# The attribute bias of an edge MLP as a 65th row of a matmul, and its relu in one instruction

## The reference, cut to what matters

```
ei   = concatenate([x[src], edge_attr], axis=-1)      # 256 + 64 values per edge
core = maximum(ei @ W1 + b1, 0.0) @ W2 + b2           # (320 x 256), then (256 x 256)
gate = sigmoid(ei @ Wg + bg)                          # (320 x 256)
agg  = segment_sum(gate * core, dst)
out  = layernorm(agg + x) * gamma + beta
```

## Time and profile before

| | |
|---|---|
| time, median of 3 runs | 3865.31 us (3860.82 to 3867.19) |
| the profiled execution | 3845.83 us, its span 3844.1 us |
| TensorE busy | 3249.5 us, 85% of the span |
| VectorE, GpSimd, ScalarE busy | 2816.0, 2085.0, 1883.4 us |
| mean granted TensorE clock | 0.925 of full speed |

### The profile page before, as it was taken

How to read it: one execution, slowest core, us unless ns; L and a number is a source line. 1 busy time by engine, 2 the same in 40 slices (tenths; PEclk the granted TensorE clock), 3 DMA queues, 4 the chain that set the end, 5 groups by cost and what they waited for, 6 DMA issues and landing times. The chain is left out here.

```text
span 3844.1 us, 56581 instructions
## 1 busy us (share of the span) xinstructions
PE 3249.5 (85%) x14868; PEld 2617.9 (68%) x14868; DVE 2816.0 (73%) x7894; ACT 1883.4 (49%) x5403; POOL 2085.0 (54%) x2118
## 2 busy tenths in 40 slices
PE   5999925588577799666999997999999999999875
PEld 4888824477465466333777775888878787878664
DVE  5666758699588466695666665898989898989742
ACT  3777715466333111132333332566666666666555
POOL 3667600376277566233333332767767676767567
PEclk8999969899799899755999998999999999999998
DMA  4788739644277222175333333887868686868665
GB/s 139 242 247 248 237 108 321 194 131 129 68 219 208 87 88 87 30 219 157 101 115 108 118 107 98 239 236 212 251 201 251 198 250 203 252 200 248 198 215 167
DMA packets 677311, 684.76 MB, mean 178 GB/s; under 512 B 73152, under 2 KB 631284, under 8 KB 676896
## 3 DMA queue, kind: packets, MB, share of 16 engines
q1 hardware_dynamic: 592456, 484.44, 40.4%
q0 software_dynamic: 68160, 181.21, 17.4%
q10 hardware_dynamic: 16380, 15.49, 1.2%
HBM read 401.66 MB, written 283.11 MB: 178 GB/s over the span
## 5 line engine op out<-in xcount | busy, mean ns | idle before, releaser
L2812 PE MATMUL s_i_bank<-s_i_messages,s_i_equal 128*128 128x256 f32 x1200 | 360.0, 383 | 5.6 <-DMA s_i_messages<-h,table_row 5.4
L621 POOL DMA_INDIRECT s_i_messages<-h,table_row x300 | 306.5, 1022 | 98.5 <-issue 78.7
L621 POOL DMA_INDIRECT s_i_messages<-h,table_row_b x300 | 308.0, 1027 | 90.1 <-issue 79.7
L931 POOL TENSOR_TENSOR n_powers<-n_powers,neg_half 128x8 f32<-128x8 f32 (+3 forms) x164 | 268.4, 1637 | 160.2 <-DVE n_powers L896 116.1
L856 ACT ACTIVATE n_z<-gamma_bc,n_powers 128x256 f32<-128x256 f32 x320 | 175.0, 594 | 362.0 <-POOL n_powers L931 362.0
L815 PE MATMUL s_n_bank<-w,n_xt 128*128 128x256 f32 x1280 | 305.7, 382 | 16.7 <-DMA n_xt<-in_x_t 16.7
L833 PE MATMUL s_n_bank<-w_out,n_ht 128*128 128x256 f32 x1280 | 313.9, 390 | 4.7 <-ACT n_ht L843 4.4
L824 PE MATMUL s_n_bank<-n_x3t,w_in 128*128 128x256 f32 x1280 | 302.5, 379 | 0.0
L2841 DVE SCALAR_TENSOR_TENSOR s_i_y<-s_i_bank,s_i_scale,acc 128x256 f32<-128x256 f32 x600 | 285.1, 476 | 0.3 <-PE s_i_bank L2812 0.2
L833 PEld LDWEIGHTS s_n_bank<-w_out,n_ht 128*128 128x128 f32 x1280 | 249.0, 196 | 46.2 <-ACT n_ht L843 11.1
L815 PEld LDWEIGHTS s_n_bank<-w,n_xt 128*128 128x128 f32 x1280 | 245.2, 192 | 51.3 <-DMA n_xt<-in_x_t 17.1
(11 more groups left out here) (448 smaller groups left out, 9244.8 us busy)
## 6 DMA issues: line engine op xcount, KB each, us to landing
h<-s_i_y SPq DMA_DIRECT2D x600, 128.0 KB, 3.9
n_xt<-in_x_t SPq DMA_DIRECT2D x160, 256.0 KB
out<-n_w SPq DMA_DIRECT2D x160, 256.0 KB
s_i_equal<-eq_tab SPq DMA_DIRECT2D x600, 64.0 KB, 3.9
x<-s_x_rows SPq DMA_DIRECT2D x100, 256.0 KB
out<-s_a_hs SPq DMA_DIRECT2D x100, 128.0 KB, 3.0
proj_dst<-s_a_hd SPq DMA_DIRECT2D x100, 128.0 KB
h<-s_h_rows SPq DMA_DIRECT2D x50, 256.0 KB, 3.7
```

The lines of the kernel that those rows point to most:

```text
L621: return net.nc.gpsimd.indirect_dma_start(out, None, table, bass.IndirectOffsetOnAxis(index, 0))
L931: self.nc.gpsimd.tensor_tensor(v[:, 8 + b0:8 + b1], v[:, b0:b1], self.net.neg_half[:, 0:b1 - b0], ALU.pow).then_inc(self.powered, 1)
L2812: nc.tensor.matmul(banks[r % 4][:, 0:D], EQ[q % NM][:], M[q % NM][:], start=True, stop=True).then_inc(summed, 1)
```

## The change

The bias of the MLP's first product goes into the product over the attributes, as it is in the gate already. `net.w_m1e` gets a 65th row, which is loaded with the bias; `hidden` multiplies it with all 65 rows of the attribute tile, whose last row is ones; the wait for those ones moves from `gate` to `hidden`. `relu` no longer has a bias, so one instruction over 512 values per partition takes the place of two over 256. The bias no longer needs its columns, and `net.cols` has two columns of biases where it had three; the list of loads keeps its 27 entries, but the entries behind `w_m1e` move by one place up to the former column load, and so change queues.

```
-        self.w_m1e = sb("w_m1e", [self.DE, D])
+        self.w_m1e = sb("w_m1e", [self.DE + 1, D])
...
-        self.col_names = ["b1", "bm1", "b_in"]
-        self.cols = sb("cols", [P, 3, C])
+        self.col_names = ["b1", "b_in"]
+        self.cols = sb("cols", [P, 2, C])
...
-            (net.w_m1[:], chunks(a["wm1"][0:D, :])), (net.w_m1e[:], a["wm1"][D:D + net.DE, :]),
+            (net.w_m1[:], chunks(a["wm1"][0:D, :])), (net.w_m1e[0:net.DE, :], a["wm1"][D:D + net.DE, :]),
+            (net.w_m1e[net.DE:net.DE + 1, :], a["bm1"].unsqueeze(0)),
...
                     past(pe, relu_ready, k)
+                    pe.wait_ge(ones_ready, NB)
...
-                        mm = nc.tensor.matmul(out, net.w_m1e[:, m * P:(m + 1) * P], at[0:DE, :], start=False, stop=True)
+                        mm = nc.tensor.matmul(out, net.w_m1e[:, m * P:(m + 1) * P], at[:, :], start=False, stop=True)
...
                     past(pe, tanh_ready, k)
-                    pe.wait_ge(ones_ready, NB)
...
-                    for m in range(C):
-                        mv = nc.scalar.activation(RL[:, m, :], hds[:, m * G * P:(m + 1) * G * P], ACT.Relu, bias=net.cols[:, 1, m:m + 1])
-                    mv.then_inc(relu_ready, 1)
+                    nc.scalar.activation(RL[:].rearrange("p c e -> p (c e)"), hds[:, :], ACT.Relu).then_inc(relu_ready, 1)
```

More of the change, by code:

```diff
@@ L353, in _ @@
         def _(sp):
-            with nc.allow_non_contiguous_dma("three biases as columns, once"):
+            with nc.allow_non_contiguous_dma("two biases as columns, once"):
                 for dst, src in keys:
@@ L842, in silu @@
         for m in range(self.C):
-            mv = self.nc.scalar.activation(self.HT[:, m, :], self.hd[:, 2 * m * P:2 * (m + 1) * P], ACT.Silu, bias=self.net.cols[:, 2, m:m + 1])
+            mv = self.nc.scalar.activation(self.HT[:, m, :], self.hd[:, 2 * m * P:2 * (m + 1) * P], ACT.Silu, bias=self.net.cols[:, 1, m:m + 1])
         mv.then_inc(self.ht_ready, 1)
```

## The result

| | before | changed |
|---|---|---|
| median time, us | 3863.07 (4 runs, 3859.90 to 3867.19) | 3823.27 (4 runs, 3818.02 to 3823.89) |
| ratio | | 0.9893, 95% interval 0.9877 to 0.9908 |
| span of the profiled execution, us | 3844.1 | 3816.3 |

The account below looks back on a forecast made before the run. TensorE, busy throughout the edge MLP stage, was taken as the bound. 49 turns at 0.78 us (38.2 us) plus 1.18 us for turn 0 gave 39.4 us; 3865.3 - 39.4 = 3825.9, say 3826 us, range 3812 to 3842.

Parts of the forecast that it names:

- The product over 65 rows: In `hidden`, replacing the 64-row attribute product removes 0.78 us a turn on TensorE, 39.4 us in all.
- The rival of the open weight loads: In `hidden`, four 65-row weight loads of 0.19 us no longer hide, 0.76 us a turn; 3864 us, chance 0.03.
- its slower sibling at 3903: In `hidden`, the gaps stay and the exposed full weight loads come on top; 3903 us, chance 0.02.
- The rival of the role: In `hidden`, the gap belongs to the product's role, not its rows, and loads stay hidden; 3865 us, chance 0.04.
- That no other engine takes over: In a turn, VectorE keeps 2.92 us idle before its join, tanh starts 0.15 us late but covered; no engine catches up.
- The case of another engine taking over for half of a turn's gain: Another engine, tanh nearest, limits part of the turn; 19 us of gain left, 3846 us, chance 0.06.
- The relu: One instruction for two saves ScalarE 0.24 to 0.26 us a turn; counted as nothing, 13 us if on the path.
- Setup: Before the stages, a row load replaces a column load and neighbours change queues; nothing, between -1 and +1 us.
- The term of turn 0: In the stage's first turn, at the 1.2 GHz clock, `hidden` loses its gaps; 1.18 us saved.
- The profiled execution: Span of the whole kernel under the profiler, claimed to go from 3845.8 to 3806.4 us.

## Why the prediction was right

The forecast was 3826 us, range 3812 to 3842, on a median of 3865.3; the time is 3823.3 on a median of 3863.1. The predicted difference was 39.4 us, the measured one 39.8. That the two agree to 0.4 us is in part luck, for by the interval the difference may be anything from 35.5 to 47.5 us; what was predicted and found sharply is the turn.

*The product over 65 rows* carried the sum, and its step held: 0.78 us a turn was predicted from the earlier trace rows and 11.17 - 10.39 = 0.78 measured. The runs with one part alone show that this is all of a turn's gain. The run with the small products side by side and the one with 64 rows in the gate show where the price sits: a visit to fewer rows costs 0.39 us at the full clock, whether it holds one such product or two, in either role. The rule of the Trainium skill that changing the tiling mode drains TensorE (TensorEngine Tiling (Array Packing), section Key Properties) fits all of these runs; that the lost time is such a drain no view names, and the runs show its size and where it stands.

*The rival of the open weight loads* would have given 3864: the 65-row loads run under the matmuls before them, so it is out, as is its slower sibling at 3903. The prediction read the rule of the other page too narrowly. The same section of the Trainium skill (TensorE: Matmul & The Clock Gate, section The mechanism) also lets a weight load go ahead where its rows don't conflict with those in use or where it goes to a background buffer for weights. The loads over 65 and 128 rows that start 0.21 to 0.22 us early agree with that sentence, and not with the one that the prediction quotes. *The rival of the role* fell with the gate at 64 rows.

*That no other engine takes over* held in its numbers: 2.92 us of idle time were foretold for VectorE and 2.92 measured. The tanh now starts behind the norm without idle time, as forecast, and nobody waits for it. Its delay was forecast at 0.15 us and is 0.05: it starts 0.20 us behind `total` before (2068.39 and 2068.19) and 0.25 behind it now (2069.22 and 2068.97):

```profile
2068.22 1.09 ACT L2583 ACTIVATE s_g_x<-s_g_z,s_g_small 128x256 f32<-128x256 f32 x2 [1.06 <-POOL s_g_small L2427]
...
2068.97 1.03 PE L2507 MATMUL s_g_bank<-s_g_messages,s_g_equal 128*128 128x256 f32 x4
```

The prediction let it wait for the end of the norm, which is at 2068.22 + 1.09 = 2069.31 us here, and the tanh starts 0.09 us ahead of that.

*The case of another engine taking over for half of a turn's gain* was put at 3846 us; its own terms, 3865.3 - 39.4 + 19.1, make 3845. It did not come.

*The relu* saves ScalarE 0.24 us (0.84 to 0.60), the lower end of what was forecast, and none of it reaches the end. The prediction set two instructions against one and did not ask what the bias costs; three quarters of the 0.24 us are the bias.

*Setup* was costed at nothing, and the run with all but the 65th row shows nothing within its interval (0.9987 to 1.0009 of 3863.6 us, so between 5.0 us less and 3.5 us more). TensorE's first use at this place starts at 19.84 us in both kernels (the earlier trace rows has the one before; here the view ended within the four records):

```profile
4.27 0.33 SPq L359 DMA_DIRECT2D w_m1e<-in_bm  x1
...
19.84 0.48 PE L393 MATMUL s_setup_bank<-ident,w1x 128*128 128x128 f32 x1 [1.56 <-DVEq L497]
```

*The term of turn 0,* 1.18 us, was right as a price and can't be found as a term. The changed kernel's products at the lower clock do stand without gaps, 0.85 us for two records and 1.70 and 1.71 for four:

```profile
1818.87 1.91 PE L2471 MATMUL s_g_bank<-s_g_xt,w_m 128*128 128x256 f32 x4
1820.57 1.06 PE L2472 MATMUL s_g_bank<-s_g_attr,w_m1e 65*128 65x256 f32 x2
1821.42 1.91 PE L2471 MATMUL s_g_bank<-s_g_xt,w_m 128*128 128x256 f32 x4
1823.13 0.99 PE L2472 MATMUL s_g_bank<-s_g_attr,w_m1e 65*128 65x256 f32 x2
```

But the stretch from the stage's first transposes to those in turn 1 took 16.5 us in the first profile of the kernel before and 16.2 in the second, and from 12.2 to 13.5 in the seven profiles of other kernels, those with 64 rows in `hidden` or gate among them (12.5 to 13.1). The granted clock is what differs: in the second ten microseconds behind the stage's first gathers it was 0.50 and 0.52 in the two profiles of the kernel before, and 0.73 to 0.91 in the seven others. Why it stayed low longer in just these two is not shown. Neither the old setup nor the 64-row products do it by themselves: the run with 32 rows has the old setup and took 12.5 us, the one with 64 rows and one relu has all four gaps and took 12.8.

*The profiled execution* was forecast at 3806.4 us and took 3818.0. That was the weakest step: it set the gain against one execution whose stages ahead had been 11 us shorter than in the changed kernel's. The stage itself, from its first gathers to those of the next stage, went from 600.2 us (1797.5 to 2397.7) to 558.3 us (1808.5 to 2366.8), 41.9 us less; in the repeats it took 599.7 and 556.9. Not all of the 41.9 us is the 65th row. The 49 turns at the full clock make 38.2; of the other 3.7 us, 3.0 lie in the stretch of turn 0 (16.5 and 13.5 us), where the visits (1.18 us by the earlier trace rows) and the later rise of the clock can't be told apart. The three other kernels with two visits a turn (64 rows and one relu, the gate at 64, 32 rows) took 596.4, 596.6 and 595.8 us for the stage, and against these the three with none (558.3, 556.9 and 558.4) are 37 to 40 us shorter. The time of the whole can't tell 38 us from 42, since the interval of the run with all but the 65th row is 8.5 us wide.

## What to carry to other kernels

When products over a full contraction of 128 rows and products over 64 or 32 rows alternate, and TensorE is what the stage waits for, count the visits: each had the same price here. A 65th row (a bias on a row of ones, say) takes it away, and an order that puts the small products side by side makes one visit of two. Only 32-bit products and these numbers of rows were tried. Read such a stage by the starts of the matmuls, since a busy share of 100% hid 0.78 of 11.17 us, 7% of the turn. And where the stages ahead scatter by more than an edit is worth, compare the turn of the stage between two profiles, not the spans.

## What the runs showed of the hardware that was not expected

A visit costs 0.39 us at the full clock and is spread over its neighbours. In the run with the small products side by side, the group of four before the visit takes 0.96 us where 0.86 is its own, the four small records 1.05 and the group of four behind them 0.97: 0.10, 0.19 and 0.11 us too much. The price is the same for 32 and for 64 rows, and for one or two products in it. A wider product (65 rows against 64) costs no time by itself. At the lower clock two visits cost 8.02 - 6.84 = 1.18 us, 0.59 us each, so the price grows by half when the clock halves. Dropping a per-partition bias took 0.09 us off each relu over 256 values, and merging the two without it 0.06 us off both together.
